# Two preact convolution layers on one core: 24 map rows a tile in one load, padded constants, and in the second pass an earlier spectrum load and two halves of contraction weights

## The reference

```
# layer 0: spectral convolution
xf  = rfft2(gn(x))                              # per image and channel
out = einsum('bhixy,hioxy->bhoxy', xf[..., :32, :17], weight)   # 4 heads of 16 channels
x   = x + irfft2(out) + bias
# layer 1: Lorentz batch norm over channels, every pixel is one point
m = mean over all pixels ; mu = m / sqrt(max(m0^2 - sum(m[1:]^2), EPS))
alpha = max(xf[:,0]*mu0 - xf[:,1:] @ mu[1:], 1+EPS) ; d = arccosh(alpha) ; var = mean(d*d)
coef  = d / sqrt(alpha^2 - 1) ; v = coef * (xf - alpha*mu) ; ...
s = gamma * vs / (sqrt(var) + EPS) + beta ; t = sqrt(1 + sum(s*s)) ; x = x + [t, s]
```

## Time and profile before

| what | value |
|---|---|
| three runs | 3991.98, 3998.57, 4014.85 us; median 3998.57 |
| profiled execution's own time | 4024.94 us |
| its span | 4023.4 us |
| PE, DVE, ACT, POOL busy | 75%, 68%, 53%, 38% of the span |
| DMA | 1199.08 MB, mean 298 GB/s |

### The profile page before, as it was taken

One profiled execution on the slowest core, in us unless ns is written; L12 is line 12 of the kernel. 1 busy time (PEld: TensorE's weight loads), 2 busy tenths in 40 slices (PEclk: granted clock), 3 DMA queues, 4 the chain that ended last, 5 costly groups with the idle time before them and its releaser, 6 DMA issues. The chain is left out here.

```text
span 4023.4 us, 77883 instructions
## 1 busy us (share of the span) xinstructions
PE 3002.5 (75%) x26018; PEld 1495.1 (37%) x26018; DVE 2748.0 (68%) x2969; ACT 2141.8 (53%) x2940; POOL 1513.6 (38%) x876
## 2 busy tenths in 40 slices
PE   6988898989446767677715877877777778877776
PEld 3555555555211222222203434344333344443332
DVE  1888888888865355555444767677777677777766
ACT  6777676767200011111014767677776677776665
POOL 0110101010111111111113766666666666666666
PEclk9988888988668888888857999999999999999999
DMA  9878777677269999999915989899999899999898
GB/s 373 287 256 282 260 265 274 244 285 253 76 259 354 325 341 376 362 361 374 334 53 183 337 313 329 313 325 321 313 315 320 306 330 334 329 334 311 311 314 288
DMA packets 280512, 1199.08 MB, mean 298 GB/s; under 512 B 35145, under 2 KB 37038, under 8 KB 197934
## 3 DMA queue, kind: packets, MB, share of 16 engines
q1 hardware_dynamic: 266126, 1152.07, 79.9%
q0 software_dynamic: 14112, 43.37, 3.4%
HBM read 883.53 MB, written 311.73 MB: 297 GB/s over the span
## 5 line engine op out<-in xcount | busy, mean ns | idle before, releaser
L1323 POOL TENSOR_TENSOR c_ot<-c_ot,c_pp 128x1024 f32<-128x1024 f32 x512 | 1211.8, 2368 | 727.0 <-DVE c_ot L1272 651.8
L1262 DVE SCALAR_TENSOR_TENSOR c_xt<-c_xt,keep_k,c_p_u 128x1024 f32<-128x1024 f32 x512 | 654.0, 1277 | 332.5 <-DMA c_xt<-in_x 170.8
L1118 PE MATMUL c_p_u<-c_mv,c_zc 64*128 64x256 f32 x4096 | 612.3, 420 | 225.1 <-DVE c_xt L1262 163.1
L1272 DVE SCALAR_TENSOR_TENSOR c_ot<-c_p_f,keep_k,c_xt 128x1024 f32<-128x1024 f32 x512 | 657.3, 1284 | 177.0 <-DMA out<-c_ot 134.4
L1198 ACT ACTIVATE c_pp<-c_p_p,c_cols 128x1024 f32<-128x1024 f32 x512 | 570.5, 1114 | 362.4 <-PE c_p_p L1132 359.0
L1205 ACT ACTIVATE c_sq<-c_xt,c_cols 128x1024 f32<-128x1024 f32 x512 | 584.2, 1141 | 139.5 <-DVE c_xt L1262 138.8
L1118 PEld LDWEIGHTS c_p_u<-c_mv,c_zc 64*128 64x128 f32 x4096 | 371.4, 195 | 532.9 <-DVE c_xt L1262 321.3
L327 ACT ACTIVATE a_junk<-a_xt 128x1024 bf16<-128x1024 f32 x512 | 537.2, 1053 | 28.8 <-DMA a_xt<-in_x 21.5
L246 PE MATMUL a_p_rows<-a_xt,a_dft_h 128*64 128x512 f32 x2048 | 517.5, 652 | 33.6 <-DMA a_bias_t<-in_bias 19.5
L1132 PE MATMUL c_p_f<-c_rt,c_lwc 64*128 64x512 bf16 x1024 | 328.0, 402 | 179.6 <-DVE c_ot L1272 161.3
L663 PE MATMUL b_p_al<-b_xt,b_awc 128*32 128x512 f32 x2048 | 312.4, 682 | 161.2 <-DMA b_xt<-in_x 116.3
(11 more groups left out here) (209 smaller groups left out, 3029.8 us busy)
## 6 DMA issues: line engine op xcount, KB each, us to landing
a_xt<-in_x SPq DMA_DIRECT2D x256, 1024.0 KB, 8.0
b_xt<-in_x SPq DMA_DIRECT2D x128, 2048.0 KB, 16.0
c_xt<-in_x SPq DMA_DIRECT2D x256, 1024.0 KB, 16.7
out<-c_ot SPq DMA_DIRECT2D x256, 1024.0 KB, 18.4
maps<-b_maps POOLq DMA_DIRECT2D x64, 192.0 KB, 5.7
dmap<-b_dmap POOLq DMA_DIRECT2D x16, 768.0 KB, 11.6
c_rt<-maps SPq DMA_DIRECT2D x512, 24.0 KB
c_dmap<-dmap SPq DMA_DIRECT2D x16, 768.0 KB, 17.2
```

The costliest lines, as they stand in the source:

```text
L1118: last = nc.tensor.matmul(p_u[:, 512 * at + W * r:512 * at + W * r + W], zc[t // CH][64 * at:64 * at + 64, i], mv[t % NB][64 * at:64 * at ...
L1262: V.scalar_tensor_tensor(out=u, in0=u, scalar=kc, in1=p_u[:], op0=ALU.mult, op1=ALU.add).then_inc(u_done, 1)
L1272: V.scalar_tensor_tensor(out=ot[t % NB][:, at], in0=p_f[:], scalar=kinv, in1=xt[t % NB][:, at], op0=ALU.add, op1=ALU.mult).then_inc(f_done, 1)
L1323: P.tensor_tensor(o, o, pp[n][:], ALU.add).then_inc(o_done, 1)
```

## The change

In pass C the 24 map rows of a tile become one DMA. The HBM tensor `maps` has now 24 rows an image, which include the repeated ones (part 1 three times, part 2 twice, part 3 once for each map and row parity), and they land on partitions 4, 9, 14, ..., 119. The two `bmap` loads stay. The masks in `misc` follow the new rows. The rows are written in pass B: POOL stores six parts as before, into every other pair of rows, and ACT stores six more (parts 1 and 2 of both maps, and part 1 of both again) in 12 DMAs an image, as the last item of its image; DVE's `dense` waits also for these. `idft_w` has 48 rows, 11 of them zeros; pass C loads all 48, pass B its 37.

In pass B `awc` has two halves, for even and odd images. DVE writes the half of image b + 1 after dense(b - 1); POOL writes the first two before the loop. `weights` is gone from POOL's order, so that its loop is load_modes(b), store_urows(b - 1), load_dense(b), store_dense(b - 1). `load_modes(0)` stands ahead of POOL's first waits.

```diff
+MAP_AT, MAP_STEP = 4, 5
+MAP_PAIRS = ((0, 2, 4), (1, 3), (5,))
...
-    iw = np.zeros((YS, W))
+    iw = np.zeros((48, W))
...
-    for at, first in ((12, 0), (18, 64)):
-        for part, (row, rows) in enumerate(((0, 6), (6, 4), (10, 2))):
-            for s in range(2):
-                m[first + row + s:first + row + rows:2, at + 2 * part + s] = 1.0
+    for a, at in enumerate((12, 18)):
+        for part, pairs in enumerate(MAP_PAIRS):
+            for pair in pairs:
+                for s in range(2):
+                    m[MAP_AT + MAP_STEP * (12 * a + 2 * pair + s), at + 2 * part + s] = 1.0
...
# pass B
-    maps_v = io["maps"].rearrange("b m s (k j n) -> b j (s k) m n", j=4, n=512)
+    maps_v = io["maps"].rearrange("b (q g s) (k j n) -> b g j (s k) q n", q=6, g=2, j=4, n=512)
...
-        aw, awc = sb("aw", [128, B, 2, 2]), sb("awc", [128, 2, 47])
+        aw, awc = sb("aw", [128, B + 2, 2, 2]), sb("awc", [128, 2, 2, 47])
...
# PE
-                pe.wait_ge(w_ready, b + 1)
+                pe.wait_ge(w_ready[par], b + 2 - par)
...
# ACT
+            def repeat_maps(b):
+                act.wait_ge(maps_ready, b + 1)
+                for j in range(4):
+                    at = slice(32 * j, 32 * j + 32)
+                    for a in (0, 3):
+                        act.dma_start(maps_v[b, 1, j, :, a:a + 2], maps[at, a:a + 2]).then_inc(again_out, 16)
+                    act.dma_start(maps_v[b, 1, j, :, 2::3], maps[at, 0::3]).then_inc(again_out, 16)
             def entry(b):
                 copy_z(b)
                 distances(b)
+                repeat_maps(b)
...
# POOL
-            def weights(b):
-                if not is_at(b, 0):
-                    pool.wait_ge(al_mm, b * T)
-                P.tensor_copy(awc[:, :, 15:47:16], aw[:, b]).then_inc(w_ready, 1)
...
-                    pool.dma_start(maps_v[b, j], maps[at]).then_inc(maps_out, 16)
+                    pool.dma_start(maps_v[b, 0, j], maps[at]).then_inc(maps_out, 16)
...
             def entry(b):
-                weights(b)
                 load_modes(b)
...
+            load_modes(0)
             pool.wait_ge(setup, 4)
...
-            weights(0)
-            load_modes(0)
+            for b in range(2):
+                P.tensor_copy(awc[:, b, :, 15:47:16], aw[:, b]).then_inc(w_ready[b], 2)
...
# DVE
                     dve.wait_ge(maps_out, b * 64)
+                    dve.wait_ge(again_out, b * 192)
...
+            def weights(b, par):
+                V.tensor_copy(awc[:, par, :, 15:47:16], aw[:, b] if isinstance(b, int) else aw[:, bass.ds(b, 1)].squeeze(1)).then_inc(w_ready[par], 2)
...
                 combine(b)
                 dense(b - 1, 1)
+                weights(b + 1, 1)
                 combine(b + 1)
                 dense(b, 0)
+                weights(b + 2, 0)
...
# pass C
-    maps_v = io["maps"].rearrange("b m s (t n) -> b t (m s) n", n=TC)
+    maps_v = io["maps"].rearrange("b r (t n) -> b t r n", n=TC)
...
+                sp.dma_start(r[MAP_AT:MAP_AT + 24 * MAP_STEP:MAP_STEP], maps_v[b, t]).then_inc(r_in[t % NB], 16)
                 for at in range(2):
-                    for row, rows in ((0, 6), (6, 4), (10, 2)):
-                        sp.dma_start(r[64 * at + row:64 * at + row + rows], maps_v[b, t, 6 * at:6 * at + rows]).then_inc(r_in[t % NB], 16)
                     sp.dma_start(m[64 * at + M2:64 * at + M2 + 2].rearrange("p (n r) -> p n r", n=2), bmap_v[b, t, at]).then_inc(r_in[t % NB], 16)
...
-                    sp.dma_start(m[64 * at:64 * at + YS].rearrange("p (r w) -> p r w", w=W), cst["idft_w"].unsqueeze(1).to_broadcast((YS, 4, W))).then_inc(c_in, 16)
+                    sp.dma_start(m[64 * at:64 * at + 48].rearrange("p (r w) -> p r w", w=W), cst["idft_w"].unsqueeze(1).to_broadcast((48, 4, W))).then_inc(c_in, 16)
...
-                    pe.wait_ge(r_in[t % NB], b * (128 * T // NB) + 128 * (t // NB) + 128)
+                    pe.wait_ge(r_in[t % NB], b * (48 * T // NB) + 48 * (t // NB) + 48)
...
-        io["maps"] = dram("maps", (B, 6, 2, HALF), BF16)
+        io["maps"] = dram("maps", (B, 24, HALF), BF16)
```

More of the change, by code:

```diff
@@ L566, in stage_b @@
     dense_v = lambda a: a.rearrange("b s (k j n) -> b j (s k) n", j=4, n=512)
-    maps_v = io["maps"].rearrange("b m s (k j n) -> b j (s k) m n", j=4, n=512)
+    maps_v = io["maps"].rearrange("b (q g s) (k j n) -> b g j (s k) q n", q=6, g=2, j=4, n=512)
     x_in = [sem(f"x_in{k}") for k in range(NX)]
-    c_in, setup, w_ready = sem("c_in"), sem("setup"), sem("w_ready")
+    c_in, setup, w_ready = sem("c_in"), sem("setup"), [sem(f"w_ready{k}") for k in range(2)]
     pow_done, mean_ready = sem("pow_done"), sem("mean_ready")
@@ L576, in stage_b @@
     e_ready, maps_ready, maps_out, beta_out, dmap_out = sem("e_ready"), sem("maps_ready"), sem("maps_out"), sem("beta_out"), sem("dmap_out")
+    again_out = sem("again_out")
     var_in, var_mm, std_ready = sem("var_in"), sem("var_mm"), sem("std_ready")
@@ L635, in _ @@
             sp.dma_start(idft_h[0:64], cst["idft_d"]).then_inc(c_in, 16)
-            sp.dma_start(idft_w[:], cst["idft_w"]).then_inc(c_in, 16)
+            sp.dma_start(idft_w[:], cst["idft_w"][0:YS]).then_inc(c_in, 16)
             sp.dma_start(ones[:], cst["sel"][:, 0]).then_inc(c_in, 16)
@@ L662, in contract @@
                             at = 2048 * half + 512 * j
-                            last = nc.tensor.matmul(out[32 * j:32 * j + 32, :], awc[:, kind, 15 - k:47 - k], xt[t % NX][:, at:at + 512],
+                            last = nc.tensor.matmul(out[32 * j:32 * j + 32, :], awc[:, par, kind, 15 - k:47 - k], xt[t % NX][:, at:at + 512],
                                                     start=(k == 0), stop=False, skip_group_check=True)
@@ L738, in _ @@
                 entry(b)
+            act.wait_ge(again_out, B * 192)
         @block.gpsimd
@@ L891, in _ @@
             ch.inc(V.memset(awc[:], 0.0))
+            ch.inc(V.memset(aw[:, B:B + 2], 0.0))
             ch.inc(V.memset(uw[:], 0.0))
@@ L910, in _ @@
                 mask = misc[:, 8 + s:9 + s].to_broadcast((128, B))
-                V.scalar_tensor_tensor(out=aw[:, :, 0, s], in0=rcol[:], scalar=mcol[:], in1=mask, op0=ALU.mult, op1=ALU.mult).then_inc(aw_ready, 1)
-                V.scalar_tensor_tensor(out=aw[:, :, 1, s], in0=keep["cols"][:, :, 0], scalar=gb[:, 1:2], in1=mask, op0=ALU.mult, op1=ALU.mult).then_inc(aw_ready, 1)
+                V.scalar_tensor_tensor(out=aw[:, 0:B, 0, s], in0=rcol[:], scalar=mcol[:], in1=mask, op0=ALU.mult, op1=ALU.mult).then_inc(aw_ready, 1)
+                V.scalar_tensor_tensor(out=aw[:, 0:B, 1, s], in0=keep["cols"][:, :, 0], scalar=gb[:, 1:2], in1=mask, op0=ALU.mult, op1=ALU.mult).then_inc(aw_ready, 1)
             ch.inc(V.tensor_scalar(s1(4), mrow[:, 0:1], 1.0, None, ALU.add))
@@ L945, in _ @@
             dense(0, 0)
+            dve.wait_ge(aw_ready, 4)
+            weights(2, 0)
             with dve.Fori(2, B - 1, 2) as b:
```

## The result

| | before | after |
|---|---|---|
| median of four runs | 3999.96 us | 3721.00 us |
| from, to | 3991.98, 4014.85 | 3713.68, 3724.43 |
| span of the profiled execution | 4023.4 us | 3717.7 us |

A forecast was written before the change was run, and what follows sets the result against it. Both passes were taken as bound by transfers most of the time, though not at full rate, with a hole at the start of C. Terms -49 - 20 + 5 - 130 = -194 took 3998.57 to 3805 us, range 3680 to 3930.

The forecast's parts named there:

- stream of B: Pass B's x stream: PE's waits removed, 42 us at most, against the cost of six more stored parts; net +5 us.
- last sign: Closing test: the prediction is wrong if C moves less than 60 or more than 200 us.
- start of C: Eight constant loads at pass C's start: 48 rows spread over the DMA engines where 37 used one; gain 49 us.
- Tiles of C: Pass C's tiles: fewer small loads on SP recover scattered DMA dips; gain 130 us, from 0 to 410.
- Between them: idle DMA time is 0.09 x 1853 = 167 us: Pass C's tiles: of this idle time 55 us at image turns stay, 110 are recovered, plus 20 for fewer DMAs.
- The other end: Pass C's tiles, upper limit: SP's issue as the whole bound gains 1.6 us a tile, 410 us over 256 tiles.
- The crowding rival: Pass C: small loads crowd one DMA engine, which sets the tile's pace; -270 us in C, time 3665; chance 0.2.
- The price of the repeats: Pass B: the added 12.6 MB of stored parts cost 30 us at 426 GB/s to 59 us at 4.7 us a MB.
- They count only where they starved the DMA engines: Pass B's stream: removed waits of PE gain only the DMA engines' idle time, (1 - 0.95) x 835 = 42 us.
- End of B: Pass B's last image: earlier spectrum load puts combine(15) inside image 14, dense(15) 22 us earlier; gain 20, between 10 and 24.
- The slower rival: Pass B: ACT's 12 stores, each waiting for the last to land, hold copy_z; +300 us, time 4100; chance 0.04.
- The second rival: Pass C: transfers are what they are, no byte is saved, so C gains nothing; time 3935; chance 0.17.

The follow-up runs named there:

- pad_only: Kernel before with only the constant of pass C, `idft_w`, padded to 48 rows; 3954.04 us, ratio 0.9896.
- tiny5: Changed kernel with five more loads a tile in pass C, each 16 rows of 32 bytes into scratch; 3977.95 us, ratio 0.9986 to the kernel before.
- rows25: Changed kernel with 25 map rows instead of 24 in the one load of a tile; 3840.08 us, ratio 0.9646 to the kernel before.
- halves_ahead: Kernel before with the `awc` halves, DVE's weights and POOL's new order, plus the next image's spectrum loaded ahead of the dense stores; 3935.33 us, ratio 0.9877.
- halves_only: Kernel before with the `awc` halves, DVE's weights and POOL's new order, maps and constant as before; 4073.27 us, ratio 1.0169.
- ahead: Changed kernel with load_modes(b + 1) placed ahead of store_dense(b - 1) in POOL's order; 3700.51 us, ratio 0.9250 to the kernel before.
- rows6x4: Changed kernel with a tile's 24 map rows loaded by six DMAs of four rows; 4188.45 us, ratio 1.0517 to the kernel before.
- rows23_1: Changed kernel with a tile's 24 map rows loaded by two DMAs, of 23 rows and of 1; 4919.29 us, ratio 1.2352 to the kernel before.
- maps_pad: Changed kernel with a single `awc` written by POOL in its old order; maps, ACT's stores and padding stay; 3930.36 us, ratio 0.9886 to the kernel before.
- ahead_pool: Changed kernel with the next spectrum loaded ahead of the dense stores and the 12 repeat stores moved from ACT to POOL; 3733.79 us, ratio 0.9381 to before.

## Why the prediction was right or wrong

The range of 3680 to 3930 held 3721, but the gain forecast was 194 us and the measured one 279. In part the terms made up for each other: the stream of B gained where a loss was forecast, and its end did not gain. By the prediction's own last sign, "wrong if C moves less than 60 or more than 200 us", the term of C failed: the tiles moved 225 us (200 against `pad_only`). Only the start of C came out as worked out.

**Start of C: right**, by its own step (-46.3 for -49; `pad_only` -46.7). PE's eight mode parts did hide the late x loads, which land at 2066.1 and 2068.7, while the first `p_u` starts at 2086.1 behind the last mode part.

**Tiles of C: the mechanism right, its size too small.** The step that failed is "Between them: idle DMA time is 0.09 x 1853 = 167 us". I took the busy share as time that nothing could give back. The share rose by only 0.03, while the rate rose by 41 GB/s: the busy engines had not been at rate. `tiny5` shows it most plainly, with a share of 0.92 while SP's issues set the pace. What the tiles gained is 200 to 225 us in place of 130. The other end, "SP gains 1.6 us a tile, 410 us over 256 tiles", came from the right instrument, but counted the 24-row load as cheap as a small one (0.77, not 0.3), and left out that SP then meets the next bound: it waits 2.58 us a tile. The crowding rival, at 0.2, named the other half of the cause. It said -270 for the tiles and 3665 in all; the crowding of `rows25` alone is worth 109. The true answer lay between my forecast and this rival because both holds were real; that it came inside the whole range owes something to luck.

**Stream of B: wrong in sign (+5, measured -39.5, and -19 against `pad_only`).** Two steps failed. The price of the repeats, 30 to 59 us, was about 26. The 4.7 us a MB of the small transfers is not far off by itself: the same working on `halves_ahead`, where the ring is cut (a share of 1.01 at 384 GB/s over 755 us, 15.3 images of 2.70 MB), gives an estimate of 4.3. But it does not carry over to the added 1 KB pieces, at 2.0; why is open. And "They count only where they starved the DMA engines" treated waits one by one. Of those said to vanish, VectorE's for `spt` stayed (332.6 us) and PE's for `zs` grew; `halves_only` removed the one for `awc` and lost 71 us. Only both parts together give the gain.

**End of B: wrong (+4.4 for -20).** The step was "combine(15) runs inside image 14 and dense(14) at the start of image 15". It did not happen: the ring above puts the spectrum behind the stores, so that combine(15) starts at 1947.6, 10 us ahead of the last x load, and dense(14) at 1961.9, behind it. The end of after:

```profile
1957.39 0.33 SPq L646 DMA_DIRECT2D b_xt<-in_x  x1
...
1983.44 3.32 ACTq L742 DMA_DIRECT2D maps<-b_maps  x1
...
1990.13 0.59 ACT L720 ACTIVATE b_zs<-b_p_z 34x512 f32<-34x512 f32 x1 [20.42 <-issue]
1991.04 2.07 PE L686 MATMUL b_p_y<-b_idft_w,b_zs 34*128 34x256 f32 x4 [19.85 <-ACT b_zs L721]
...
2001.93 0.75 DVE L850 TENSOR_SCALAR b_dn<-b_p_al,b_ac 128x512 f32<-128x512 f32 x1 [25.07 <-PE b_p_ls L667]
```

dense(15) starts 44.5 us after the last x load is issued, against 43.1 before (2038.94 in the earlier trace rows, load at 1995.8). PE's last two tiles stand behind `zs`, and ACT comes to copy it only when the maps of dense(14) are made and its twelve stores are issued, at 1989.6. `ahead`, which does load the spectrum an image early, gained 22 us at this place: the size that I had given was that of another kernel. Its dense(15) starts 22.2 us after the last x load:

```profile
1980.03 0.75 DVE L853 TENSOR_SCALAR b_dn<-b_p_al,b_ac 128x512 f32<-128x512 f32 x1 [20.79 <-DMA maps<-b_maps]
```

**The slower rival** had the right place and the wrong price. The twelve issues took 5.7 us in most images, as the prediction had it, and 13.0 at the end. But they wait for the maps of the dense step, and so `copy_z` behind them is held by more than the issues (199.8 us in 14 images, up to 20.4), and PE stands 12 to 20 us in the images read. Four x buffers cover it at a share of 0.97. Only at the end of B does it show.

**The second rival**, no gain in C, is ruled out by the tiles. Its ground, a high share, was the one that failed in my own term.

**What stays open.** Why the spectrum lands later in `halves_only` (23.1 us) than before (16.1) or after (13.2): a burst of x loads released just ahead of it would do it, and in after PE stands at that moment, waiting for `zs`, and releases none. That was argued from the order and not tested. Open too are the 16 to 41 us of C that neither part alone gives, the split inside `rows6x4`, and why the share stays at 0.92 in `tiny5`.

## What to carry to other kernels

Count the issuing queue as an engine: add up, for one tile, how long it stands in issues and how long in waits. If it hardly waits, look whether its issues are as short as in a free stretch. If they are, the queue sets the pace; if they are stretched, something behind it does its part. A "DMA busy" share at a rate well below the best window is no proof of a transfer bound. Before crediting a prefetch, follow the buffer through every engine until you are back at the load. If the path closes and the DMA share is well under 1, suspect the ring and cut it: that gave 153 us in `halves_only` at 0.89. At 0.98 it gave nothing in the stream and 22 us at the end. Put small loads on a number of rows that spreads: 37 rows in place of 48, 25 in place of 24, and 23 and 1 in place of 24 each cost time here.

## What the runs showed of the hardware

- An issue on SP took from 0.25 to 0.78 us by its shape in C: 0.35 for a two-row load of `bmap` and 0.58 for 16 rows of 32 bytes (both with the gap to the next), 0.60 for four stepped rows, 0.77 for 24 stepped rows, 0.36 for 1 MB on 128 rows. Bytes did not set it; in `tiny5` eight small issues, five of them of 16 rows, bound a tile of 2.2 MB.
- A DMA share of 0.92 went with 308 GB/s in `tiny5` and one of 0.95 with 361 in after, in the same pass with the same bytes of x and output.
- In `rows23_1` a queue with one crowded engine held SP for 6.7 to 7.4 us in the issue of one row behind it, with the DMA share at 0.14.
- The landing of the same 296 KB load, issued by POOL, varied from 10.5 us (`maps_pad`) to 31.9 us (`ahead_pool`).
- The 12.6 MB of stores in 1 KB pieces cost about 2.0 us a MB of pass B at a share of 1.01 (`ahead` against `halves_ahead`).
